# Attention layer on one core: TensorE's loop without filler matmuls, fillers in the last block, and another order of the work in two steps

## The reference, cut to what matters

```python
xn = layernorm(x)
q, k, v = heads(xn, Wq, bq), heads(xn, Wk, bk), heads(xn, Wv, bv)   # 16 heads of 8
attn = softmax(q @ k.T * scale)                                     # 512 x 512 for each head
s = (attn @ v) @ Wp.T + bp
h = silu(xn @ wg.T) * (xn @ wu.T)                                   # 384 hidden
g = silu(h @ wd.T)
x = x + s * g
```

## Time and profile before

| | us |
|---|---|
| median of three runs | 1589.7 (1583.72 to 1591.99) |
| the profiled execution | 1592.2 |
| its span, first to last instruction | 1590.4 |
| PE busy | 1304.3 (82%) |
| DVE busy | 1031.1 (65%) |
| ACT busy | 869.9 (55%) |
| POOL busy | 553.7 (35%) |

### The profile page before, as it was taken

The page is one execution under the profiler, slowest core; times in us unless marked ns, Lnnn a source line. Parts: engine busy times, 40 slices in busy tenths (PEclk is TensorE's granted clock), DMA queues, the critical chain, the costliest instruction groups (busy, mean ns, idle before and its releaser), DMA issues. The chain is left out here.

```text
span 1590.4 us, 30375 instructions
## 1 busy us (share of the span) xinstructions
PE 1304.3 (82%) x8202; PEld 676.7 (43%) x8202; DVE 1031.1 (65%) x2496; ACT 869.9 (55%) x1682; POOL 553.7 (35%) x543
## 2 busy tenths in 40 slices
PE   5888998998998998998998898364676389999970
PEld 2433433433433333333343332133343278888860
DVE  1777877877877877877877781054556345545447
ACT  0277776776777777777676775212233144444432
POOL 2122232232232332332332221236555434445440
PEclk9999999999999999999999997555888789999995
DMA  6322202212212212211221300026988422222229
GB/s 225 105 71 107 103 33 88 102 52 67 102 53 66 102 53 70 98 57 66 100 82 39 107 11 13 13 76 229 283 271 269 146 61 68 67 67 69 67 59 317
DMA packets 109858, 160.12 MB, mean 101 GB/s; under 512 B 17489, under 2 KB 47761, under 8 KB 109394
## 3 DMA queue, kind: packets, MB, share of 16 engines
q1 hardware_dynamic: 100242, 141.14, 27.7%
q0 software_dynamic: 8448, 17.58, 3.2%
q10 hardware_dynamic: 1088, 0.54, 0.1%
HBM read 104.20 MB, written 49.77 MB: 97 GB/s over the span
## 5 line engine op out<-in xcount | busy, mean ns | idle before, releaser
L447 DVE TENSOR_REDUCE row_max<-ps_max 128x2 f32<-128x1024 f32 x512 | 623.0, 1221 | 187.5 <-PE ps_max L632 185.0
L599 ACT ACTIVATE probs<-ps_exp 128x512 f32<-128x512 f32 x1024 | 559.1, 602 | 266.2 <-PE ps_exp L632 260.5
L632 PE MATMUL ps_exp<-q_op,k_op 32*128 32x512 f32 x1024 | 320.3, 503 | 22.3 <-ACT probs L599 22.3
L632 PEld LDWEIGHTS ps_exp<-q_op,k_op 32*128 32x128 f32 x1024 | 139.2, 184 | 366.1 <-ACT probs L599 302.8
L712 PE MATMUL ps_y<-probs,v_aug 128*32 128x512 f32 x2048 | 279.7, 619 | 1.2 <-ACT probs L599 1.2
L632 PE MATMUL ps_max<-k_op,q_op 32*128 32x512 f32 x1024 | 253.0, 495 | 2.9 <-DMA k_op<-k_parts_scratch 2.2
L1475 ACT ACTIVATE hidden<-ps_h,b 128x256 f32<-128x256 f32 x268 | 118.6, 473 | 148.1 <-PE ps_h L1452 148.1
L1518 POOL DMA_INDIRECT y_scratch<-result,goes_to x134 | 128.3, 958 | 144.8 <-DVE result L1503 128.4
L1371 POOL DMA_INDIRECT sorted_scratch<-rows,place x128 | 123.5, 965 | 106.8 <-DVE place L1279 69.8
L351 POOL TENSOR_TENSOR rstd<-var_eps,minus_half 128x4 f32<-128x4 f32 x32 | 32.4, 1013 | 318.3 <-DVE var_eps L442 318.3
L1459 PE MATMUL ps_o<-w,hidden 128*128 128x128 f32 x1072 | 132.2, 277 | 0.0
(11 more groups left out here) (160 smaller groups left out, 1471.3 us busy)
## 6 DMA issues: line engine op xcount, KB each, us to landing
toep<-k_pad_scratch SPq DMA_DIRECT2D x32, 1024.0 KB
q_op<-q_parts_scratch SPq DMA_DIRECT2D x16, 1024.0 KB, 5.7
k_op<-k_parts_scratch SPq DMA_DIRECT2D x16, 1024.0 KB, 8.5
unit_rows<-sorted_scratch SPq DMA_DIRECT2D x136, 66.0 KB
q_parts_scratch<-q_hi SPq DMA_DIRECT2D x16, 512.0 KB, 3.1
k_parts_scratch<-k_hi SPq DMA_DIRECT2D x16, 512.0 KB, 2.8
q_parts_scratch<-q_lo SPq DMA_DIRECT2D x16, 256.0 KB, 2.4
k_parts_scratch<-k_lo SPq DMA_DIRECT2D x16, 256.0 KB, 2.1
```

The source lines that it names most:

```text
L447: dve.tensor_reduce(row_max[group // 2][:, t, head:head + 2], ps_max[u][:, :, :], AX.X, ALU.max)\
L599: act.activation(probs[s % 2][:, i, :], ps_exp[i % 2][:, :], ACT.Exp).then_inc(exp_done, 1)
L632: return pe.matmul(out, lhsT, rhs, start=True, stop=True)
```

## The change

Four edits, all in PE's program. The fillers inside `xnT`, `max0` and `max1` are left to the head alone. In the first block `max1` keeps two fillers and its place ahead of `second_group`; in all others `max1` now comes behind `second_group`, as the other side work does. In the step of `g0` the side work now comes ahead of `second_group`, in every block but the last. In the last block each of the 14 steps without side work gets one filler, behind `second_group`, which waits for `ps_side` to be free.

```diff
                 elif what == "xnT":
-                    keep_awake()
+                    if isinstance(n, int) and n < len(HEAD_SIDE):
+                        keep_awake()
...
                 elif what[0:3] == "max":
-                    keep_awake()
+                    if isinstance(n, int) and n < len(HEAD_SIDE):
+                        keep_awake()
...
-                    if s != SIDE.index("max1"):
+                    late = s == SIDE.index("g0") and exists(b + 1) or s == SIDE.index("max1") and is_first(b)
+                    if not late:
                         second_group()
                     if s in (STEPS - 3, STEPS - 2) and has_side(b, STEPS - 1):
                         begin_down(b + 1, side(b, STEPS - 1), s - (STEPS - 3))
                     elif has_side(b, s):
                         what = SIDE[s]
-                        if what == "max1":
+                        if what == "max1" and is_first(b):
                             wait(pe, side_free, side(b, s))
                             keep_awake()
+                            keep_awake()
                         to_side(what, b + of(what), par if of(what) % 2 == 0 else 1 - par, side(b, s))
-                    if s == SIDE.index("max1"):
+                    elif not exists(b + 1):
+                        wait(pe, side_free, side(b, s))
+                        keep_awake()
+                    if late:
                         second_group()
```

## The result

The changed kernel took 1580.95 us (median of 19 runs, 1560.94 to 1587.74) against 1591.99 for the kernel before (19 runs, 1583.72 to 1606.53) on the same chips. The ratio is 0.987, with a 95% interval of 0.983 to 0.991; it leaves out five slow executions of the changed kernel, over 1.5% above its fastest, with which the two medians give 0.993. I had forecast 1543, a ratio of 0.971. The profiled execution took 1587.74, the longest of the 19, with a span of 1585.9.

The account below looks back on a forecast made before the run. A ring of PE (`weigh_values`, scores) and ACT (exponentials), 3.09 us at least, bounds each step. The loop's 34.3 us and the last block's 12.4 make 46.7 off 1589.7: 1543.0 us, range for 8 in 10 1530 to 1561.

Parts of the forecast that it names:

- the last block: Block without a following one: fillers hold the clock at 1.00, 63.5 us becomes 51.1, gain 12.4, of which 1.9 from `max1`.
- the gain in an undisturbed block: Blocks 1 to 13 of the loop, with all four edits: each gets 2.49 us shorter.
- the wait for `v_aug` ahead of `g0`: Step of `g0`: PE waits for ACT with scores 2 and 3 queued behind, so `u0` starts 1.26 us later.
- the second layer beginning earlier: Behind the last block: PE idles for `yT` anyhow, so the second layer begins as before, only earlier.
- The clock in the loop: Loop, from the end of `u1` to `g2`, some 5 us with only transposes full-width: clock stays up, nothing put down.
- second rival: Loop, around `max1`: the clock dips once in each block, 1.47 x 14 = 21 us, time 1564; 7 in 100.
- The row that it leaned on: Start of the last block, 946 to 957: no fillers, scores with maxima only, clock 1.00; taken as nearest to the loop.
- the 34.3 that I had put down for the loop: Whole loop: 32.4 us from blocks 1 to 13, 2.09 from block 14, 0.21 lost in block 0.

Follow-up runs that it names:

- e4: The kernel before with only `g0` moved ahead of `second_group`, all fillers of the loop kept; ratio 1.025.
- e8: The kernel before without the loop's fillers, all orders kept, no fillers in the last block; ratio 0.987.
- e1: The changed kernel with one edit undone, `g0` again behind `second_group`; ratio 0.964.
- e9: e1 with 64 semaphore increments on PE ahead of all other work, which move the loop's exit; ratio 0.959, median 1578.1 us.
- e12: e1 run once more, on the same chip as e9 to measure it by; ratio 0.965, median 1586.2 us.
- e10: The changed kernel with 64 semaphore increments on PE ahead of all other work; ratio 0.983.
- e2: The changed kernel with one filler of 384 columns put into PE's pause ahead of `g0`; ratio 0.976.
- e5: The changed kernel run again unchanged, beside the kernel before on another chip; ratio 0.983.

## Why the prediction was wrong

Right, with sizes: the last block (12.8, forecast 12.4, of which the fillers 10.8 against 10.5); the gain in an undisturbed block (2.4 against 2.49); the wait for `v_aug` ahead of `g0` with its full length in the path (1.20 against 1.26, by e4 59.43 - 58.24 = 1.19); the second layer beginning earlier by as much as the last block ended earlier (13.0 and 12.8).

The step that failed is the one headed "The clock in the loop", which put down nothing. Two things were wrong in it.

- It looked for a fall at `max1` alone. I had worked out under g0 that PE now stands idle for 1.2 us and then waits again for ACT, priced that as waiting time, and never asked what it does to the clock. That is where the clock falls. My second rival had the size nearly right (1.47 a block, measured 1.0 to 2.2) but the wrong place and 7 in 100.
- The row that it leaned on (946 to 957, no side work, clock 1.00) was not the nearest one. PE's pauses there are single ones of some 0.5 to 0.7 us. e8 shows falls at `max1` with two pauses in a row, so those fillers had done something for the clock after all. With `max1` behind `second_group` nothing was lost by that (e1).

In the profiled execution this makes up the whole loop. Nine blocks of the loop and the last but one of the layer, with a fall of about 2.2 each, are 22 us, the block at the exit is 9.5 over 55.8 (a fall at `g0` and the pause), and the one behind that is some 1.4 over: 33 of the 34.3 that I had put down for the loop. The second miss, the pause behind the exit, had no term at all. By e9 against e12 it is worth 7.3 in the block; the medians differ by 8.1, which holds scatter too, since in the two profiles the head before the loop was 2.7 longer in e9 and the second layer 2.4 shorter. No row of before showed the pause, for before did not have it.

What is left open: why in some executions each block has a fall and in others every second or none. Once a fall has made a block 58.0 long, the next falls at the same place in the block, and so on to the end of the loop; in e10 long and short blocks alternate. One might put the wide spread of the changed kernel down to this: e9, without falls in the loop, spreads over 5 us in six runs and e10, with them, over 23 on the same chip. But e2, whose profile has no fall in the loop, spreads over 25, the kernel before over 23, and e8, with falls, over 9. So the runs don't show that link. The scatter of the second layer wasn't looked into.

The best version is e9: `g0` left behind `second_group`, all else of the change, and the exit moved. Its ratio is 0.959, against 0.987 and, in e5, 0.983 for the change as made, on other chips.

## What to carry to other kernels

A pause that you price as waiting time must be priced a second time for what it does to TensorE's clock: go through each new wait of the engine, not only through the places where work was taken out. Fillers belong where the engine waits, and one filler in the pause (e2) did what the fillers elsewhere (e4) could not. When a loop on the chip gets shorter or longer, look at the first step behind its exit, and compare the distances of equal steps over the whole run rather than one typical block.

## What was not expected of the hardware

The clock fell in pauses of 1.14 and 0.67 us with matmuls between them, while the engine counted as busy 92 of 100 us. TensorE stood still for 4.5 to 6.7 us just behind a loop's exit, always at the same instruction of 256, and 64 idle instructions ahead of it made the pause go. 232 semaphore increments went from 0.7 to 36.6 us, 0.15 us each. They put off the first matmul by no more than 24 us, since it had waited for its data until 12.2 before; the 64 of e9, inside that wait, put off nothing (12.12).
